# Mixture-of-experts layer of a decoder: every token through all eight experts, against rows sorted by expert in blocks of 128

## What is computed

```python
B, S, F, E, K = (4, 128, 128, 8, 2)
gate_probs = jax.nn.softmax(x @ Wg + bg, axis=-1)
_, top_idx = jax.lax.top_k(gate_probs, k)
expert_mask = jax.nn.one_hot(top_idx, gate_probs.shape[-1], dtype=gate_probs.dtype).sum(-2)
selected = gate_probs * expert_mask
selected = selected / (selected.sum(-1, keepdims=True) + 1e-08)
h = jax.nn.gelu(jnp.einsum('bsf,efh->bseh', x, W1) + b1)
expert_out = jnp.einsum('bseh,ehf->bsef', h, W2) + b2[None, None]
return jnp.einsum('bsef,bse->bsf', expert_out, selected)
```

## Time and profile before

| | |
|---|---|
| median of the runs | 896.72 us (890.34 to 899.08, 3 runs) |
| the profiled execution's own time | 893.9 us |
| its span, first to last instruction | 892.1 us |
| mean granted TensorE clock | 0.906 of full speed |
| TensorE matmul / VectorE / ScalarE / GpSimd busy | 84% / 56% / 48% / 16% of the span |
| DMA, mean over the span | 16 GB/s |

### The profile page before, as it was taken

How to read it: one execution, slowest core, us unless ns; L and a number is a source line. 1 busy time by engine, 2 the same in 40 slices (tenths; PEclk the granted TensorE clock), 3 DMA queues, 4 the chain that set the end, 5 groups by cost and what they waited for, 6 DMA issues and landing times. The chain is left out here.

```text
span 892.1 us, 18624 instructions
## 1 busy us (share of the span) xinstructions
PE 748.5 (84%) x7194; PEld 576.2 (65%) x7194; DVE 501.7 (56%) x1210; ACT 428.3 (48%) x861; POOL 145.3 (16%) x232
## 2 busy tenths in 40 slices
PE   3896999899998699989999994779999984675675
PEld 2464555656665589779999994557878772453554
DVE  3454554787787555232321215575757544777995
ACT  6463666687665453423444441435354424652332
POOL 3122222444442000000000003131413220000000
PEclk9798999999999669999999998699999996756787
DMA  3000011111100300000000000000000001000000
GB/s 88 2 19 18 4 30 41 49 39 46 50 13 8 125 1 1 1 1 1 1 0 0 1 1 1 0 2 2 2 1 2 2 1 24 13 4 2 4 21 24
DMA packets 17567, 14.43 MB, mean 16 GB/s; under 512 B 6691, under 2 KB 14316, under 8 KB 17485
## 3 DMA queue, kind: packets, MB, share of 16 engines
q1 hardware_dynamic: 16189, 12.39, 4.7%
q10 hardware_dynamic: 1296, 0.92, 0.4%
HBM read 11.34 MB, written 1.05 MB: 14 GB/s over the span
## 5 line engine op out<-in xcount | busy, mean ns | idle before, releaser
L922 ACT ACTIVATE experts_h<-bank,b 128x512 f32<-128x512 f32 x128 | 86.0, 689 | 100.1 <-PE bank L867 100.0
L945 DVE SCALAR_TENSOR_TENSOR x<-bank,experts_sel,x 128x128 f32<-128x128 f32 (+1 forms) x128 | 36.1, 344 | 151.6 <-PE bank L875 151.6
L875 PEld LDWEIGHTS bank<-w,experts_h 128*128 128x128 f32 x1024 | 119.0, 192 | 2.5
L875 PE MATMUL bank<-w,experts_h 128*128 128x128 f32 x1024 | 119.4, 275 | 0.0
L519 ACT ACTIVATE l_probs<-bank 128x512 f32<-128x512 f32 x128 | 66.1, 602 | 96.3 <-PE bank L432 96.2
L1296 POOL COPY ptx<-over_pt 32x512 f32<-32x512 f32 x64 | 39.0, 610 | 127.9 <-DVE over_pt L1266 125.1
L865 PE MATMUL bank<-xt_hi,w_hi 128*128 128x512 f32 (+1 forms) x128 | 53.7, 420 | 0.8 <-PEq L751 0.8
L673 DVE SCALAR_TENSOR_TENSOR l_probs<-l_probs,bank 128x512 f32<-128x512 f32 x64 | 41.1, 684 | 23.4 <-PE bank L441 21.6
L428 PE MATMUL bank<-l_qxx,l_front 32*128 32x512 f32 x256 | 37.4, 651 | 19.2 <-issue 15.5
L658 DVE TENSOR_REDUCE l_m<-bank 128x4 f32<-128x512 f32 x64 | 40.9, 679 | 20.4 <-PE bank L416 20.4
L866 PE MATMUL bank<-xt_lo,w_hi 128*128 128x512 f32 (+1 forms) x128 | 50.9, 398 | 0.0
(11 more groups left out here) (284 smaller groups left out, 1660.8 us busy)
## 6 DMA issues: line engine op xcount, KB each, us to landing
w<-in_w SPq DMA_DIRECT2D x16, 256.0 KB
x<-in_x SPq DMA_DIRECT2D x4, 256.0 KB, 3.8
out<-x SPq DMA_DIRECT2D x4, 256.0 KB, 2.3
l_cb<-in_ctx SPq DMA_DIRECT2D x16, 48.0 KB, 2.6
cos_cb<-in_ctx SPq DMA_DIRECT2D x8, 96.0 KB, 2.0
over_w<-in_over_wq SPq DMA_DIRECT2D x1, 512.0 KB
over_w<-in_over_wk SPq DMA_DIRECT2D x1, 512.0 KB
over_w<-in_over_wv SPq DMA_DIRECT2D x1, 512.0 KB
```

The source lines that it names most:

```text
L875: mm = nc.tensor.matmul(down_bank[e % 2][:, j * S:(j + 1) * S], h[e % 2][:, c, j * S:(j + 1) * S], M.w2[:, e, c, :], start=(c == 0), stop= ...
L922: nc.scalar.activation(h[e % 2][:, c, :], up_bank[c][:, :], ACT.Gelu_apprx_tanh, bias=M.b1[:, e, c:c + 1]).then_inc(s["h"], 1)
```

## The change

`route_block` takes the place of `gate_block`. It works in quarters of four tiles: VectorE finds the two best experts of each token (`choose`), TensorE counts with small matmuls how many earlier tokens chose the same expert (`rank`), and VectorE makes of it the row of a table `slots` in DRAM (`place`). GpSimd sends each tile's 128 rows (128 features, position, two weights, token number) twice through an indirect DMA into `slots`, 32 DMAs in all. `slots` has a region of 2048 rows for each expert. `blocks()` then works out for 39 blocks of 128 rows which expert each belongs to and where it begins. 39 blocks are enough for any choice of experts.

So that rows that no token fills can be told, SyncE writes a blank pattern over all of `slots` during the attentions, in 16 DMAs of 8 times 128 rows of 528 bytes (540 KB each) and a last one.

`expert_block` runs over the 39 blocks. SyncE reads the block's row and expert into registers, fetches the 128 rows from `slots` (68 KB) and copies the expert's weights and biases, 4624 bytes per partition (592 KB), from `M.w` to one of four buffers `wb` inside SBUF. TensorE turns the rows and does 4 matmuls up and 4 down, all float32 and of 128 columns. The split into high and low parts is gone. GpSimd sends the weighted results to one of two tables in DRAM by an indirect DMA, which drops the blank rows. At the end SyncE reads both tables back (8 DMAs of 256 KB), and VectorE adds them to `M.x`. The gaps' work (`fp4_step` and the splits) is now laid out one instruction per block.

Layer 0's SyncE stream and the loads:

```diff
+        eng.dma_start(M.w[:, :, B2:B2 + D], d["gate_b2"].rearrange("(a e) c -> a e c", a=1).broadcast_to([128, E, D])).then_inc(sem, 16)
     elif part <= E:
-        eng.dma_start(M.w1[:, part - 1, :], d["w1"][:, part - 1, :]).then_inc(sem, 16)
+        eng.dma_start(M.w[:, part - 1, W1:W1 + 512], d["w1"][:, part - 1, :]).then_inc(sem, 16)
     elif part <= 2 * E:
-        eng.dma_start(M.w2[:, part - E - 1, :, :], d["w2"][:, part - E - 1, :, :]).then_inc(sem, 16)
+        eng.dma_start(M.w[:, part - E - 1, W2:W2 + 512], d["w2"][:, part - E - 1, :, :].rearrange("p c d -> p (c d)")).then_inc(sem, 16)
 
 
...
                         M.cross_weights.load(sp, d, s["cross_weights"])
                     if t >= 8:
                         load_experts(sp, M, d, s["next"], t - 8)
+                    if 2 <= t < 18:
+                        sp.wait_ge(s["blank"], 4)
+                        sp.dma_start(M.slots[0:E * REGION, :].rearrange("(q n p) c -> q p n c", n=8, p=S)[t - 2],
+                                     M.blank[:, :].rearrange("p (a c) -> p a c", a=1).broadcast_to([S, 8, ROW])).then_inc(s["filled"], 16)
+                    if t == 18:
+                        sp.dma_start(M.slots[E * REGION:, :], M.blank[:, :]).then_inc(s["filled"], 16)
                 sp.wait_ge(s["next"], 16 * (5 + 2 * E))
+                sp.wait_ge(s["filled"], 16 * 17)
```

GpSimd makes the blank pattern at t = -2 (one memset of 128x132, an iota, a memset and a copy of one column, `make_blank`). The new stage, cut to its core:

```diff
-def gate_block(nc, M, d):
+def route_block(nc, M, d):
...
+                def rank(q):
+
+
+                    o = rank_bank[q % 2][:, 0:4 * E].rearrange("p (j e) -> p j e", e=E)
+                    wait(pe, s["ready"], q, plus=-1)
+                    wait(pe, s["mask"], q, plus=1)
+                    nc.tensor.matmul(o, before[:, :], mask[:, 4 * q:4 * q + 4, :], start=True, stop=False, skip_group_check=True)
+                    for b in range(4 * q):
+                        nc.tensor.matmul(o, all_ones[:, :], mask[:, b:b + 1, :].broadcast_to([S, 4, E]), start=False, stop=False, skip_group_check=True)
+                    for k in range(3):
+                        mm = nc.tensor.matmul(o[:, k + 1:4, :], all_ones[:, :], mask[:, 4 * q + k:4 * q + k + 1, :].broadcast_to([S, 3 - k, E]),
+                                              start=False, stop=k == 2, skip_group_check=True)
+                    mm.then_inc(s["rank_ps"], 1)
...
+                nc.gpsimd.iota(counting[:, 55:56], pattern=[[1, 1]], base=0, channel_multiplier=1).then_inc(s["consts"], 1)
+                nc.gpsimd.iota(counting[:, 56:72], pattern=[[S, 16]], base=B * S, channel_multiplier=1).then_inc(s["consts"], 1)
+                for q in range(NB):
+                    pool.wait_ge(s["ready"], q + 1)
+                    for j in range(4):
+                        for k in range(2):
+                            nc.gpsimd.indirect_dma_start(M.slots, bass.IndirectOffsetOnAxis(pos[:, k, 4 * q + j:4 * q + j + 1], 0),
+                                                         M.xs[:, 4 * q + j, :], None).then_inc(s["scattered"], 16)
+                pool.wait_ge(s["scattered"], 16 * 2 * B)
 
...
+                def best_of(k):
+
+
+                    order = M.falling[:, :].rearrange("p (a e) -> p a e", a=1).broadcast_to([S, 4, E])
+                    then(V.tensor_reduce(best[:, k, :, 0], p[:, :, :], AX.X, ALU.max))
+                    then(V.tensor_tensor(ties[:, :, :], p[:, :, :], wide(best[:, k, :, :]), ALU.is_equal))
+                    then(V.tensor_tensor(ties[:, :, :], ties[:, :, :], order, ALU.mult))
+                    then(V.tensor_reduce(r1[:, :, 0], ties[:, :, :], AX.X, ALU.max))
+                    then(V.tensor_tensor(pair[:, k, :, :], ties[:, :, :], wide(r1[:, :, :]), ALU.is_equal))
+
...
+                def choose(q):
+                    tile = slice(4 * q, 4 * q + 4)
+                    zq = logit_bank[q % 2][:, 0:4 * E].rearrange("p (j e) -> p j e", e=E)
+                    wait(dve, s["logit_ps"], q, plus=1)
+                    then(V.tensor_reduce(r1[:, :, 0], zq, AX.X, ALU.max))
+                    V.tensor_tensor(z[:, :, :], zq, wide(r1[:, :, :]), ALU.subtract).then_inc(s["shifted"], 1)
+                    if q == 0:
+                        constants()
+                    if q + 2 < NB:
+                        normalise(q + 2)
+                    wait(dve, s["exps"], q, plus=1)
+                    then(V.tensor_reduce(r1[:, :, 0], p[:, :, :], AX.X, ALU.add))
+                    then(V.reciprocal(r1[:, :, 0], r1[:, :, 0]))
+                    then(V.tensor_tensor(p[:, :, :], p[:, :, :], wide(r1[:, :, :]), ALU.mult))
+                    best_of(0)
+                    then(V.scalar_tensor_tensor(p[:, :, :], pair[:, 0, :, :], -2.0, p[:, :, :], ALU.mult, ALU.add))
+                    best_of(1)
+                    V.tensor_tensor(mask[:, tile, :], pair[:, 0, :, :], pair[:, 1, :, :], ALU.add).then_inc(s["mask"], 1)
+                    then(V.scalar_tensor_tensor(r1[:, :, 0], best[:, 0, :, 0], 1e-8, best[:, 1, :, 0], ALU.add, ALU.add))
...
+                def place(q):
+                    rq = rank_bank[q % 2][:, 0:4 * E].rearrange("p (j e) -> p j e", e=E)
+                    tile = slice(4 * q, 4 * q + 4)
+                    wait(dve, s["rank_ps"], q, plus=1)
+                    then(V.tensor_tensor(ranks[:, :, :], rq, start_of[:, :].rearrange("p (a e) -> p a e", a=1).broadcast_to([S, 4, E]), ALU.add))
+                    then(V.tensor_tensor(pair[:, :, :, :], pair[:, :, :, :],
+                                         ranks[:, :, :].rearrange("p (a j) e -> p a j e", a=1).broadcast_to([S, 2, 4, E]), ALU.mult))
+                    then(V.tensor_reduce(posf[:, :, :], pair[:, :, :, :], AX.X, ALU.add))
+                    then(V.tensor_copy(M.xs[:, tile, 128], posf[:, 0, :]))
+                    V.tensor_copy(pos[:, :, tile], posf[:, :, :]).then_inc(s["ready"], 1)
+
```

`blocks()` is 14 further VectorE instructions of the same kind on at most 273 elements per partition. The expert stage, the new side:

```diff
+                for j in range(J):
+                    wait(sp, s["dest"], j, plus=-3)
+                    wait(sp, s["sum"], j, plus=-3)
+                    row = sp.value_load(M.block_row[0:1, j:j + 1], min_val=0, max_val=E * REGION)
+                    e = sp.value_load(M.block_expert[0:1, j:j + 1], min_val=0, max_val=E - 1)
+                    sp.dma_start(xb[j % 4][:, :], M.slots[bass.ds(row, S), :]).then_inc(s[f"x{j % 4}"], 16)
+                    sp.dma_start(wb[j % 4][:, :], M.w[:, bass.ds(e, 1), :]).then_inc(s[f"w{j % 4}"], 16)
+                for n in range(4):
+                    sp.wait_ge(s[f"y{n}"], 16 * ((J + 3 - n) // 4))
+                for q in range(NB):
+                    for k in range(2):
+                        sp.dma_start(both[k][:, 4 * q:4 * q + 4, :],
+                                     M.results[2048 * k + 512 * q:2048 * k + 512 * q + 512, :].rearrange("(b p) d -> p b d", p=S)).then_inc(s[f"both{q}"], 16)
...
+                turn(0)
+                for j in range(J + 1):
+                    if j + 1 < J:
+                        turn(j + 1)
+                    if j < J:
+                        up(j)
+                    if j > 0:
+                        down(j - 1)
...
+                for j in range(J):
+                    wait(act, s["up"], j, plus=1)
+                    wait(act, s["down"], j, plus=-1)
...
+                        nc.scalar.activation(h[j % 2][:, c, :], up_bank[j % 2][:, c * S:(c + 1) * S], ACT.Gelu_apprx_tanh,
+                                             bias=wb[j % 4][:, B1 + c:B1 + c + 1]).then_inc(s["h"], 1)
...
+                for j in range(J):
+                    pool.wait_ge(s["weighted"], j + 1)
+                    nc.gpsimd.indirect_dma_start(M.results, bass.IndirectOffsetOnAxis(dest[j % 4][:, 0:1], 0), y[j % 4][:, :], None,
+                                                 bounds_check=2 * B * S - 1, oob_is_err=False).then_inc(s[f"y{j % 4}"], 16)
...
+                def aim(j):
+
+
+                    wait(dve, s[f"y{j % 4}"], j // 4, per=16)
+                    wait(dve, s["weighted"], j)
+                    then(V.tensor_scalar(is_first[:, :], xb[j % 4][:, 128:129], M.slot_row[:, j:j + 1], None, ALU.is_equal))
+                    V.tensor_scalar(dest[j % 4][:, :], is_first[:, :], -float(B * S), xb[j % 4][:, 131:132], ALU.mult, ALU.add).then_inc(s["dest"], 1)
+                    then(V.tensor_scalar(weight[:, :], is_first[:, :], xb[j % 4][:, 129:130], xb[j % 4][:, 130:131], ALU.mult, ALU.add))
+                    wait(dve, s["dest"], j, plus=1)
+
+                def weigh(j):
+                    wait(dve, s["down"], j, plus=1)
+                    V.tensor_tensor(total[:, :], down_bank[j % 2][:, 0:D], wb[j % 4][:, B2:B2 + D], ALU.add).then_inc(s["sum"], 1)
+                    wait(dve, s["sum"], j, plus=1)
+                    V.tensor_scalar(y[j % 4][:, :], total[:, :], weight[:, :], None, ALU.mult).then_inc(s["weighted"], 1)
...
+                turned(0)
+                for j in range(J + 1):
+                    if j + 1 < J:
+                        turned(j + 1)
+                    k = j - 2
```

(16 more changed lines are left out.)

371 lines of the change are left out of this document (179 added, 192 removed).

## The result

The changed kernel takes 867.71 us in the median (866.02 to 870.21, 4 runs), the kernel before in the same comparison 894.66 (890.34 to 899.08). The ratio is 0.970, with a 95% interval of 0.966 to 0.974: 27 us, or 3%, faster. Predicted were 872 us, within 832 to 935.

What follows compares the result with a forecast made beforehand. TensorE alone was taken to bound the expert stage. 31.6 us gained less 7 lost in layer 0 gave 24.6, so the profiled 893.9 became 869.3; the median, 2.8 higher, was 872 us, range 832 to 935.

Steps and rivals of the forecast that it cites:

- What bounds the kernel now: Expert stage before the change: bound by TensorE alone, busy 213.05 of 222.5 us; less work shortens it until something else ends last.
- TensorE per block: Expert stage: 8 float32 matmuls and a transpose per block, 2.0 us at full clock, 3.7 us at the low level.
- the mean of 3.4: Expert stage: 3.4 us per block, mean of SyncE's 3.1 and TensorE's low-clock 3.7, since MLP stretches change clock; 132.6 us.
- ScalarE, VectorE, GpSimd: Expert stage, per block: ScalarE 1.4 us at 0.35 per gelu, VectorE 2.6 at worst and later 1.6, GpSimd's scatter 1.2.
- SyncE: Expert stage: two DMA issues, two register reads at 0.7 us each and arithmetic, 3.1 us per block, bounds 1.9 to 6.3.
- The first block and the tail: Expert stage: 6 us before the first block; 17.3 us after the last period for last results, read-back and additions.
- The route stage: Routing ahead of the expert stage: first positions at 319.5, GpSimd's 32 scatters of 1.2 us end last, at 360.2.
- Layer 0: Blank writes during the attentions: mostly fit free time, 7 us lost, 4 of them at t = 3; bounds 0 to 32.
- Dear scatters: Rival, route stage: each of 32 scatters takes 3.5 us, total 950 us; decides from 2.0 us per scatter; chance 0.12.
- Slow copies: Rival, expert stage: copies inside SBUF are the bound, 4.4 us per block instead of 3.4, total 915 us; chance 0.14.
- Full clock: Rival, expert stage: TensorE keeps full clock, register reads are cheap, VectorE bounds at 2.6 then 2.0 us; 831 us; chance 0.15.
- Blank writes: Rival, layer 0: the writes hold up the attentions by 2 us per step, 32 instead of 7, total 897 us; chance 0.11.

Runs made afterwards that it cites:

- e9: The changed kernel with six buffers, one register read per block and no range checks on the two values: 827.7 us, period 2.10 us per block.
- e3: The changed kernel with one register read per block fetching both row and expert: 865.1 us, period 3.17 us as in the changed kernel.
- e5: The changed kernel with six buffers for rows and weights instead of four: 860.2 us, period 2.92 us.
- e7: The changed kernel with six buffers and one register read per block: 841.8 us, period 2.46 us.
- e1: The changed kernel with each block's row and expert as constants, so SyncE reads no register: 838.9 us, period 2.51 us.
- e4: The changed kernel with GpSimd waiting for all four quarters before its first scatter: 883.3 us in one run, period 3.21 us.
- e12: The changed kernel once more, not edited: 873.8 us in one run, period 3.19 us.
- e8: The changed kernel with each of layer 0's 16 blank writes followed by another into a table nothing reads: 884.7 us in one run.
- e2: The changed kernel with only half of the expert's weights copied from the fifth block on: 860.0 us in one run, period 3.01 us.
- e10: e9 with a quarter's four bias matmuls in the route stage made one of 32 columns: 823.7 us, 4.0 less than e9.

## Why the prediction was right or wrong

**What bounds the kernel now: right.** TensorE's work fell from 213 to 85 us, and something else ended last.

**TensorE per block: right at the full clock.** 2.0 us were predicted; at the period of 2.10 that e9 reaches it has 1.96 us of work. The 3.7 us of the low level, and with them the mean of 3.4, were wrong. The granted clock stayed at 1.00 from 382 us to the end of the blocks, with TensorE busy for only 38.71 of 60 us. The argument from the MLP's stretches did not carry over.

**ScalarE, VectorE, GpSimd: right.** The gelu took 368 ns (0.35), the small ones of VectorE 0.21 to 0.29, the scatter of results 1.03 us, and none of the three ended last.

**SyncE: right in size, wrong in what follows from it.** 3.1 us were predicted and 2.9 measured, with reads of 0.30 and 0.65 us in the median where I took 0.7 for each. The Trainium skill (DMA: Bandwidth & Descriptors, Latency and other measured facts) gives such a load a floor of about 600 ns; the first read of a block lies under it, at 0.26 us at its quickest, and so does e3's single one with a median of 0.49.

The step that failed is this sentence: "Four buffers are in flight, so only its rate counts and not the landing." TensorE's order holds two of the four, and the landing is in a ring with SyncE's reads. The ring makes 3.17 us of SyncE's 2.9 (e5, with six buffers, has 2.92), and it takes away what a cheaper SyncE would give: 0 us in e3 in place of 0.46 (e5 to e7). TensorE does wait in every block, as the prediction has it, but for the rows and never for the weights. That the rate of SyncE alone gives nearly the same made the error invisible in the total. It took e3, e5 and e7 together to see it.

**The first block and the tail: too short by 2 and 3 us.** The first `up` starts 7.0 us after the stage does, since `turn(1)` stands ahead of it on TensorE and its rows are asked for only in SyncE's second round, at 373.11. It then runs at the low clock (1.92 us in place of 1.06). In the tail I counted the transfer and only the last quarter's additions. But VectorE needs 2.85 us per quarter, more than a quarter's share of the reads, so all four stand in a row in the timeline of the changed kernel:

```profile
505.05 5.34 SPq L1030 DMA_DIRECT2D experts_both<-results  x8
508.86 1.42 DVE L1144 TENSOR_TENSOR x<-x,experts_both 128x512 f32<-128x512 f32 x2 [6.83 <-DMA experts_both<-results]
...
511.72 1.41 DVE L1144 TENSOR_TENSOR x<-x,experts_both 128x512 f32<-128x512 f32 x2
```

**The route stage: right in its mechanism, 7 us short.** The first positions were ready at 319.4 (319.5 predicted), and GpSimd ended last with scatters near 1.2 us. 4.0 us are a pause of GpSimd that nobody could read from the trace of before and that e1 to e4 do not have, 2.1 are 32 times 0.065, and the rest is the barrier after the landing, where I took 0.8 us and it was 2.

**Layer 0: wrong, 0 in place of 7 us.** The wait at t = 3 grew from 6.63 to 7.89 us, not by 4, and in this profile the stage's end did not move. The same layer 0 ended at 305.2 in e12 and at 306.6 in e5, so 0 to 4 us is what the runs show. Why so little is not shown. The mechanism exists, as e8 shows, but its full price begins where the queue has no room left.

**The rivals.** Dear scatters: no, 1.265 us against the 2.0 from which it decides, with VectorE busy for 28.79 us beside them. The rule of the Trainium skill (SBUF — State Buffer, SBUF: two separate sides) on descriptors that wait for VectorE's copies named 3.1 us; the scatters here took 0.96, beside VectorE's instructions of 0.2 to 0.3. Slow copies: no, e2. Full clock: the clock came, the cheap reads didn't, so its 831 us were reached only by e9. Blank writes: no. Even two sets (e8) cost 15.8 us and not this rival's 32, and e8 took 884.7 us where the rival has 897.

## What to carry to other kernels

Buffers in flight are counted where an in-order engine stands and waits, not where they are declared: follow one buffer from its request through every instruction ahead of its release, and divide the whole time by the blocks that this spans. Where two limits lie close together, neither edit alone shows its worth, so try both before giving one up. And where a new stage feeds an engine that issues one DMA after another, its first issue sets the end: what stands ahead of it counts in full, and what stands beside it counts nothing until it ends last itself, as the block table does in e10.
